# Two layers of cross-attention with experts: the softmax computed on keys-by-queries scores, built batch by batch

## Chip, cores and metric

One core of one Trainium2 chip runs the whole program in one launch. The metric is the device time of one execution in microseconds (us).

## The reference, cut to what matters

Two layers run one after the other on `x` (16 batches of 128 tokens, width 256). Each layer is a cross-attention with a residual, then a mixture of experts with a residual. The change touches only the attention:

```python
# per layer: h = layernorm(x)
# q = h @ Wq.T + bq ; k, v = ctx @ Wk.T + bk, ctx @ Wv.T + bv   16 heads of 16; layer 0 turns q and k by rope
# s = q @ k.T / 4                      per batch and head: 128 queries x 128 keys
# layer 1: s = where(mask == 0, -big, s)   over keys
# x = x + softmax(s) @ v @ Wo.T + bo
```

Results have to hold fp32 accuracy, which is why products are made of a high and a low part of each operand.

## The kernel before, in words

**Staging.** A layer's attention works in four blocks of four batches (`N` = 512 tokens). Groups are numbered i = 0 to 15 in a block: group i is four heads (two per half `u`) of batch i // 4. Engines are programmed by hand, each with its own order, and meet by semaphores; `attend(n, build)` exists once for each engine (TensorE L1386, ScalarE L647, VectorE L1056, GpSimd `outputs` L445).

**Path of one group.** `scores` (L1328) multiplies queries by keys, K = 32 rows at a time, in fp32, into banks 0 to 3; two heads of a 32-row stripe are told apart by `k_half`, which holds the keys twice, each time with the other head's rows at zero. In layer 1 a product with `mask_b` adds the mask (L1352). `shifted` (L1027, VectorE) takes the maximum over keys, negated, and for even groups also adds it to the scores (L1037). `exps` (L627, ScalarE) takes the exponential: in one instruction for even groups, and in four with the maximum as bias for odd ones (L636). `turned` (L1358) transposes the four 128x128 blocks on TensorE (L1364). ScalarE copies them to a high half in fp16 (L654), VectorE makes the low half (L1063), and `weighed` (L1368) multiplies both by the values, which are split in three bf16 parts and carry a column of ones (`VW` = 50 columns a head), into banks 6 and 7. ScalarE copies the sums out (L644), VectorE takes the reciprocal of the denominator (L1043), GpSimd adds the three parts and divides (L453 to L458).

**Blocks.** The last four groups of a block also build the next block's keys and queries (`unit`, L1301), GpSimd does the last step of rope (L443), and after them come the values (L1317). In layer 0 every key or query unit needs two products, one with the weights and one with the weights of the partner column. At a block's end all its outputs are transposed (L1406), split (L668, L1076), multiplied by Wo and added to `xres` (L1086). `attend` is a hardware loop on ScalarE, VectorE and GpSimd.

Of the kernel before, what the change touches and what calls it, by code (L numbers as in the profile page):

```python
# [18 lines left out]
VW = 50  # L19
RING, RINGT = 6, 3  # L20
# [15 lines left out]
def program(nc, x, ctxT, maskrow, tab_in, ident_in, aw, ab, arow, rw, rrow, fw, sort_in, empty_in, sorted_x, summed, out):  # L36
# [7 lines left out]
    with ctx:  # L44
# [20 lines left out]
        first_row = sb(ctx, "first_row", [P, P], BF16)  # L65
        mask_b = sb(ctx, "mask_b", [P, B * S], BF16)
        half_col = sb(ctx, "half_col", [P, 2], F32)
# [24 lines left out]
        aw_hi = sb(at, "aw_hi", [P, 6, KT, D], F32R)  # L92
        aw_lo = sb(at, "aw_lo", [P, 6, KT, D], F32R)
        rope_b = sb(at, "rope_b", [P, 2, N], F32)
        qk = sb(at, "qk", [P, 2, N], F32)
        k_half = sb(at, "k_half", [P, KT, 2, N], F32)
        q_full = sb(at, "q_full", [P, KT, N], F32)
        gap = sb(at, "gap", [P, 7 * 1024], F32)
        v32 = sb(at, "v32", [P, 2, 2, D], F32)
        v_parts = sb(at, "v_parts", [P, BLK, HEADS, VW], BF16)  # L100
        gap2 = sb(at, "gap2", [P, 2 * 1024], F32)
        probT_hi = sb(at, "probT_hi", [P, RINGT, N], F16)
        probT_lo = sb(at, "probT_lo", [P, RINGT, N], F16)
        nmax = sb(at, "nmax", [P, 2, HEADS], F32)
        rden = sb(at, "rden", [P, 2, HEADS // 2], F32)
        o_raw = sb(at, "o_raw", [P, 2, HEADS // 2, VW], F32)
        o_sb = sb(at, "o_sb", [P, BLK, HEADS, HD], F32)
        oT_hi = sb(at, "oT_hi", [P, KT, N], F32R)
        oT_lo = sb(at, "oT_lo", [P, KT, N], F32R)
        st = ExitStack()  # L110
        prob = sb(st, "prob", [P, RING, N], F32)
        st.close()

# [50 lines left out]
        s_half = sem("s_half")  # L164
# [4 lines left out]
        s_rope = sem("s_rope")  # L169
        s_wsplit = [sem(f"s_route_split{l}") for l in range(2)]  # L170

        def stage_sems(names, l):
# [5 lines left out]
                          "proj", "qk", "kfirst", "ksecond", "vps", "v32", "vhi", "vones", "vres", "vmid", "vlo",  # L178
                          "score", "max", "sub", "exp", "pT", "phi", "plo", "pv", "ocopy", "oadd", "rden", "olast",
                          "o", "oT", "ohi", "olo", "wo", "xadd", "xbo"], l)  # L180
# [16 lines left out]
        NW = [6, 4]  # L197
        JT = [2, 1]


        V_W, O_W = [4, 2], [5, 3]
        W_ORDER = [[2, 3, 0, 1, 4, 5], [1, 2, 0, 3]]
        KV_WEIGHTS = 2
        UNIT_W = [[(2, 3), (2, 3), (0, 1), (0, 1)], [(1,), (1,), (0,), (0,)]]
        GROUPS = BLK * NG
# [10 lines left out]
        def four_by_two(c):  # L216
            return (o_raw[:, c % 2].rearrange("p (u m) w -> p u m w", u=2),
                    o_sb[:, c // 2].rearrange("p (u c m) d -> p c u m d", u=2, c=2)[:, c % 2])
# [5 lines left out]
        def _(sp):  # L224
# [6 lines left out]
            sp.dma_start(aw_raw[:, 0, :], aw[0][:, W_ORDER[0][0], :]).then_inc(AT[0]["aw_in0"], 16)  # L231
            sp.dma_start(aw_raw[:, 1, :], aw[0][:, W_ORDER[0][1], :]).then_inc(AT[0]["aw_in1"], 16)
# [15 lines left out]
            for l in range(2):  # L248
# [6 lines left out]
                for i, w in enumerate(W_ORDER[l]):  # L255
# [4 lines left out]
                    sp.dma_start(aw_raw[:, i % 2, :], aw[l][:, w, :]).then_inc(a[f"aw_in{i % 2}"], 16)  # L260
# [22 lines left out]
                sp.wait_ge(a["xadd"], 2 * NBLK)  # L283
# [36 lines left out]
        def _(pool):  # L320
# [91 lines left out]
            for r in range(NG):  # L412
                nc.gpsimd.memset(first_row[32 * r:32 * r + 1, :], 1.0).then_inc(s_set, 1)
# [7 lines left out]
            for l in range(2):  # L421
# [23 lines left out]
                def outputs(n, build):  # L445

                    for c in range(2 * BLK - 1):
                        if build and l == 0:
                            for i in {4: (0,), 5: (1, 2), 6: (3,)}.get(c, ()):
                                rotate(n + 1, i)  # L450
# [1137 lines left out]
```

## Time and profile before

| | us |
|---|---|
| median of 3 runs | 1118.29 (1117.19 to 1121.87) |
| the profiled execution | 1119.13 |
| its span, first to last instruction | 1117.3 |
| first scores to last residual, layer 0 | 49.1 to 233.5 |
| first scores to last residual, layer 1 | 600.6 to 772.1 |
| TensorE matmul busy, of the span | 952.8 (85%) |
| VectorE, ScalarE, GpSimd busy | 776.6, 581.0, 436.6 |
| mean granted TensorE clock | 0.940 of 2.4 GHz |

Busy shares are means over stages with different limits. TensorE's matmuls overlap in the records (each lasts until its result is written), so the time from one start to the next tells more than the mean of one. Some matmul records can be missing. A fp32 matmul that isn't a transpose stands as two instructions in the trace: the four products of a `scores` call are eight records.

### The profile page before, as it was taken

How to read it: one execution, taken by the hardware profiler on the slowest of the kernel's cores; microseconds unless marked ns; L12 is line 12 of the kernel's file. 1: busy time of each engine (PE TensorE's matmuls, PEld its weight loads, DVE VectorE, ACT ScalarE, POOL GpSimd, SP SyncE). 2: the span in 40 equal slices, each digit the busy share in tenths (PEclk: the TensorE clock that was granted, in tenths of full speed). 3: DMA queues.
4: the chain of work that ended last, by engine and by line, in shares of the span. 5: the costliest groups of instructions: out<-in, count | busy, mean ns of one | idle time of the engine just before them, and what ended most of it. 6: DMA issues, size and time to landing. Idle time of an engine off the chain costs nothing.

```text
span 1117.3 us, 20415 instructions
## 1 busy us (share of the span) xinstructions
PE 952.8 (85%) x6981; PEld 825.7 (74%) x6981; DVE 776.6 (70%) x1538; ACT 581.0 (52%) x1112; POOL 436.6 (39%) x479
## 2 busy tenths in 40 slices
PE   2798878748987999999837888885989999999995
PEld 2577667536877999999825767665678888888885
DVE  5688787866664777777655687795686666667665
ACT  5375675745234667667546877874622232322221
POOL 1465556240663666666415444334012212212210
PEclk9989999859998999999956899996899999999999
DMA  3300750010325888888540000001000001000002
GB/s 129 110 21 1 189 144 1 1 61 1 128 82 193 237 231 233 227 221 233 119 134 1 20 20 1 1 2 43 15 15 29 28 14 28 17 26 28 14 0 76
DMA packets 44281, 85.81 MB, mean 77 GB/s; under 512 B 4161, under 2 KB 31041, under 8 KB 44097
## 3 DMA queue, kind: packets, MB, share of 16 engines
q0 software_dynamic: 14784, 46.44, 15.1%
q1 hardware_dynamic: 29440, 38.61, 11.9%
q8 instruction: 37, 0.61, 0.2%
q14 instruction: 20, 0.16, 0.0%
HBM read 64.25 MB, written 20.79 MB: 76 GB/s over the span
## 4 chain that ended last, share of the span: by engine, by line
PE 48%; DVE 20%; ACT 11%; issue 9%; DMA 7%; POOL 4%; DVEq 0%; ACTq 0%; POOLq 0%
PE bank L1179 31%; PE bank L1215 8%; DMA w_raw<-in_fw,w_idx 4%; DVE nmax L1034 3%; PE bank L1274 3%; DVE probT_lo L1063 2%; PE bank L1364 2%; DVE prob L1037 2%; POOL sorted_x L375 2%; ACT xn L512 2%; DMA summed<-y_sb,tile_to 2%; ACT probT_hi L654 1%; ACT o_raw L644 1%; PE bank L1343 1%; ACT w_hi L533 1%
## 5 line engine op out<-in xcount | busy, mean ns | idle before, releaser
L1179 PE MATMUL bank<-xT_hi,w_hi 128*128 128x512 f32 x352 | 139.9, 398 | 2.2 <-DVE hid L964 2.2
L581 ACT ACTIVATE act_sb<-bank 128x512 f32<-128x512 f32 x88 | 52.6, 598 | 167.8 <-PE bank L1179 167.7
L1179 PE MATMUL bank<-xT_lo,w_hi 128*128 128x512 f32 x352 | 139.3, 396 | 0.0
L1179 PE MATMUL bank<-xT_hi,w_lo 128*128 128x512 f32 x352 | 139.1, 395 | 0.0
L964 DVE TENSOR_TENSOR hid<-bank,act_sb 128x512 f32<-128x512 f32 x88 | 60.8, 691 | 107.3 <-ACT act_sb L581 107.1
L332 POOL TENSOR_TENSOR w_hi<-w_raw,zero_col 128x768 fp32r<-128x768 f32 (+1 forms) x20 | 31.9, 1595 | 262.9 <-PE bank L1215 236.8
L951 DVE SCALAR_TENSOR_TENSOR xres<-bank,gate,xres 128x256 f32<-128x256 f32 x320 | 132.6, 476 | 0.8 <-PE bank L1215 0.8
L1364 PE MATMUL bank<-ident,prob 128*128 128x128 f32 x512 | 86.2, 298 | 31.9 <-DVE probT_lo L1063 26.0
L1063 DVE TENSOR_TENSOR probT_lo<-bank,probT_hi 128x512 f16<-128x512 f32 x128 | 88.0, 687 | 32.4 <-ACT probT_hi L654 31.8
L1179 PE MATMUL bank<-xsT_hi,w_hi 128*128 128x256 f32 x368 | 106.5, 289 | 2.3 <-DVE xsT_lo L918 1.5
L1215 PE MATMUL bank<-w_hi,hid_hi 128*128 128x256 f32 x352 | 99.5, 283 | 6.2 <-DVE hid_lo L972 6.2
L1179 PE MATMUL bank<-xsT_hi,w_lo 128*128 128x256 f32 x368 | 103.4, 281 | 0.0
L586 ACT ACTIVATE hid_hi<-hid 128x512 fp32r<-128x512 f32 x88 | 55.7, 633 | 91.7 <-PE bank L1215 53.7
L1179 PE MATMUL bank<-xsT_lo,w_hi 128*128 128x256 f32 x368 | 103.3, 281 | 0.0
L1364 PEld LDWEIGHTS bank<-ident,prob 128*128 128x128 f32 x512 | 60.7, 150 | 56.5 <-issue 29.6
L1215 PE MATMUL bank<-w_hi,hid_lo 128*128 128x256 f32 x352 | 99.6, 283 | 0.0
L1215 PE MATMUL bank<-w_lo,hid_hi 128*128 128x256 f32 x352 | 99.3, 282 | 0.0
L394 POOL DMA_INDIRECT summed<-y_sb,tile_to x46 | 84.7, 1842 | 21.1 <-DMA summed<-y_sb,tile_to 10.9
L1034 DVE TENSOR_REDUCE nmax<-bank 128x4 f32<-128x512 f32 x128 | 85.7, 675 | 8.4 <-PE bank L1352 6.0
L654 ACT ACTIVATE probT_hi<-bank 128x512 f16<-128x512 f32 x128 | 77.3, 604 | 19.5 <-PE bank L1364 19.2
L359 POOL DMA_INDIRECT w_raw<-in_fw,w_idx x46 | 49.8, 1083 | 94.8 <-ACT y_sb L550 35.2
L533 ACT ACTIVATE w_hi<-w_raw 128x1536 fp32r<-128x1536 f32 x46 | 68.2, 1484 | 33.4 <-DMA w_raw<-in_fw,w_idx 33.3
(199 smaller groups left out, 2763.5 us busy)
## 6 DMA issues: line engine op xcount, KB each, us to landing
w_raw<-in_fw SPq DMA_DIRECT2D x18, 384.0 KB, 3.0
sorted_x<-empty_row SPq DMA_DIRECT2D x2, 2967.0 KB, 21.4
xs<-sorted_x SPq DMA_DIRECT2D x23, 258.0 KB, 3.4
ctx_raw<-in_ctxT SPq DMA_DIRECT2D x8, 512.0 KB, 5.2
aw_raw<-in_aw SPq DMA_DIRECT2D x10, 256.0 KB, 3.8
summed<-empty_row SPq DMA_DIRECT2D x1, 2304.0 KB, 29.6
xres<-in_x SPq DMA_DIRECT2D x4, 512.0 KB, 5.7
xn_all<-summed SPq DMA_DIRECT2D x4, 512.0 KB, 5.9
```

The source lines that it names most:

```text
L394: nc.gpsimd.indirect_dma_start(out=summed, out_offset=bass.IndirectOffsetOnAxis(ap=tile_to[:, j, c:c + 1], axis=0), in_=y_sb[:, j % 2, c, ...
L533: nc.scalar.activation(w_hi4[s][:], w_raw4[s], ACT.Copy).then_inc(TS["w_hi"], 1)
L581: nc.scalar.activation(act_sb[:, (ls * J + j) % 2, :], bank[2 * ((ls * J + j) % 2) + 1][:], ACT.Silu).then_inc(f["act"], 1)
L586: nc.scalar.activation(hid_hi[:, ls % 2, j, :], hid[:, (ls * J + j) % 2, :], ACT.Copy).then_inc(f["hhi"], 1)
L654: nc.scalar.activation(probT_hi[:, i % RINGT, :], bank[4 + i % 2][:], ACT.Copy).then_inc(a["phi"], 1)
L951: nc.vector.scalar_tensor_tensor(out=rows, in0=bank[4 + 2 * (ls % 2) + sub // 2][:, D * (sub % 2):D * (sub % 2 + 1)], scalar=gate[:, ds(it ...
L964: nc.vector.tensor_tensor(hid[:, r, :], bank[2 * r][:], act_sb[:, r, :], ALU.mult).then_inc(f["hid"], 1)
L1034: nc.vector.tensor_reduce(mx, grp, AX.X, ALU.max, negate=True).then_inc(a["max"], 1)
L1063: nc.vector.tensor_tensor(probT_lo[:, i % RINGT, :], bank[4 + i % 2][:], probT_hi[:, i % RINGT, :], ALU.subtract).then_inc(a["plo"], 1)
L1179: last = nc.tensor.matmul(dst, lh, rh, start=(i == 0), stop=(i == len(pairs) - 1))
L1215: last = nc.tensor.matmul(dst, h, w, start=(i == 0), stop=(i == len(pairs) - 1))
L1364: last = nc.tensor.transpose(bank[4 + i % 2][:, S * h:S * (h + 1)], prob[:, i % RING, S * h:S * (h + 1)], ident[:])
```

## The change

The softmax's second half no longer transposes probabilities. Scores are computed twice: queries by keys only for the maximum, and keys by queries, onto which TensorE itself adds the negated maximum before the exponential. The probabilities come out already turned, and the values are the stationary operand, 32 columns a head in fp32. Work goes by batch (16 steps and two to drain), unrolled on every engine; keys, queries and values of a later block are built two items a step. In layer 0 the partner product is gone: VectorE exchanges neighbouring rows instead.

```diff
+        def build_at(b):
+            early = {0: (1, K0, K1), 1: (1, Q0, Q1), 2: (1, V0, V1)}
+            if b in early:
+                return early[b]
+            n, s = divmod(b, BLK)
+            if s == 3 and n + 2 < NBLK:
+                return n + 2, K0, V0
+            if s == 0 and n + 1 < NBLK:
+                return n + 1, K1, V1
+            if s == 1 and n + 1 < NBLK:
+                return n + 1, Q0, Q1
+            return None
...
 # SP: one more load
+                sp.dma_start(mask_col[:], maskrow.rearrange("o (b t) -> (o t) b", t=S),
+                             allow_slow_non_contiguous=True).then_inc(s_in, 16)
...
 # GpSimd: outputs, value_parts gone; clears v_full (8 x 16 x 32 a partition) and low_col in each layer
+                nc.gpsimd.memset(v_full[:], 0.0).then_inc(a["vset"], 1)
+                nc.gpsimd.memset(v_full[:, :, :, :, HD], 1.0).then_inc(a["vset"], 1)
...
 # ScalarE
+                def attend():
+                    context_high(1)
+                    low_copy(0)
+                    for b in range(B + 2):
+                        if b < B:
+                            exponential(b, 0)
+                            exponential(b, 1)
+                        if 1 <= b <= B:
+                            output_copy(b - 1)
+                        if b < B:
+                            exponential(b, 2)
+                            exponential(b, 3)
+                        if b >= 2:
+                            output_high(b - 2)
+                        made, before = build_at(b), build_at(b - 1) if b else None
+                        for item in before[1:] if before and l == 0 else ():
+                            if item not in (V0, V1):
+                                unit_out(before[0], item)
+                        for item in made[1:] if made and l == 1 else ():
+                            if item not in (V0, V1):
+                                unit_out(made[0], item)
+                        if b in (2, 5):
+                            context_high(2 + b // 4)
+                        if b + 1 < B:
+                            low_copy(b + 1)
...
 # VectorE
+                    dve.wait_ge(a["rope"], 3 * u + 2)
+                    nc.vector.stream_shuffle(rope_b[:, r], rope_b[:, r], PAIR).then_inc(a["rope"], 1)
...
+                def attend():
+                    lowest(0)
+                    for b in range(B + 2):
+                        if b + 1 < B:
+                            lowest(b + 1)
+                        if b >= 2:
+                            output_low(b - 2)
+                        made = build_at(b)
+                        if made:
+                            made_item(made[0], made[1])
+                        if 1 <= b <= B:
+                            output(b - 1)
+                        if b >= 2:
+                            residual(b - 2)
+                        if made:
+                            made_item(made[0], made[2])
...
 # TensorE, scores(b): queries by keys, then the mask in layer 1
+                    if b >= 1:
+                        pe.wait_ge(a["lowcopy"], b)
+                    if b >= 3:
+                        pe.wait_ge(a["o"], b - 2)
...
+                    for u in range(KT):
+                        for h in range(2):
+                            for r in range(NG):
+                                rows = slice(32 * r, 32 * r + 32)
+                                at_col = 256 * u + S * h
+                                last = nc.tensor.matmul(bank[r][:, at_col:at_col + S], q_half[rows, n % 2, u, h, cols],
+                                                        k_full[rows, n % 2, u, cols], start=(u == 0 and h == 0),
...
 # scores_turned(b): waits for all exponentials of b-1 and for VectorE's reads of banks 4 and 5
+                    if b >= 1:
+                        pe.wait_ge(a["exp"], NG * b)
...
+                            nc.tensor.matmul(bank[4 + r][:, 256 * u:256 * u + 256], k_full[rows, n % 2, u, cols],
+                                             q_half[rows, n % 2, u, :, cols], start=(u == 0), stop=False)
+                    pe.wait_ge(a["lowcopy"], b + 1)
...
+                            last = nc.tensor.matmul(bank[4 + r][:, S * h:S * (h + 1)], pick[rows, h, :],
+                                                    low_row[rows, b % 2, :], start=False, stop=(h == GRP - 1))
...
 # weighed(b)
+                    for pair in range(2):
+                        for u in range(KT):
+                            for q in range(4):
+                                r, j = 2 * pair + q // 2, q % 2
+                                last = nc.tensor.matmul(bank[0][32 * q:32 * q + VW, S * (2 * u + pair):S * (2 * u + pair + 1)],
+                                                        v_full[:, n % 2, c, 8 * u + 2 * r + j, :],
+                                                        prob[:, b % 2, r, S * (2 * u + j):S * (2 * u + j + 1)],
+                                                        start=True, stop=True)
...
+                def attend():
+                    scores(0)
+                    lows_turned(0)
+                    for b in range(B + 2):
+                        made = build_at(b)
+                        if b + 1 < B:
+                            scores(b + 1)
+                        if b < B:
+                            scores_turned(b)
+                        if 1 <= b <= B:
+                            weighed(b - 1)
+                        if b >= 2:
+                            output_turned(b - 2)
+                        if made:
+                            pe.wait_ge(a["exp"], NG * b + 1)
+                            make_item(made[0], made[1])
+                        if 1 <= b <= B:
+                            turned_back(b - 1)
+                        if b >= 2:
+                            projected(b - 2)
+                        if made:
+                            pe.wait_ge(a["exp"], NG * b + 2)
+                            make_item(made[0], made[2])
+                        if b + 1 < B:
+                            lows_turned(b + 1)
```

What the new names stand for. `lowest` (VectorE): four maximum reductions of a bank of 512 columns. `lows_turned`: one transpose of the maxima; `low_copy` (ScalarE): a copy of 128 columns. `exponential` (ScalarE): one bank of 512 columns, with a bias column. `output_copy` (ScalarE): bank 0, 512 columns. `turned_back`: four transposes. `output` (VectorE): a reciprocal of 16 columns and a product of 256. `output_turned`: two transposes; `output_high` (ScalarE), `output_low` (VectorE): 256 columns; `projected`: six products of 256 columns; `residual` (VectorE): 256 columns. A key or query unit is six products of 512 columns on TensorE; in layer 0 VectorE follows with two operations of 512 columns and the shuffle, GpSimd subtracts, and for queries ScalarE writes two copies of 512 columns (`unit_out`); in layer 1 ScalarE writes a key unit with one and Q1 with two, VectorE Q0 with two. A value item is twelve products of 256 columns and two additions of 256 on VectorE.

## Rows read from the trace of the kernel before

**Rows 1.** The page: busy time by engine, and the chain's shares by engine
```profile
PE 952.8 (85%) x6981; PEld 825.7 (74%) x6981; DVE 776.6 (70%) x1538; ACT 581.0 (52%) x1112; POOL 436.6 (39%) x479
PE 48%; DVE 20%; ACT 11%; issue 9%; DMA 7%; POOL 4%; DVEq 0%; ACTq 0%; POOLq 0%
```
**Rows 2.** The chain in order of time: start, us, what; first piece of blocks
```profile
122.88 2.81 PE bank L1179 x12
168.88 2.81 PE bank L1179 x12
...
632.89 1.66 PE bank L1179 x6
641.02 2.97 PE bank L1179 x24
...
674.01 1.66 PE bank L1179 x6
```
**Rows 3.** Windows: stretch, length, busy us and instructions by engine, PEclk, DMA
```profile
138.50:184.50 46.00, 38.41 (x361) 31.77 (x362) 37.75 (x69) 29.67 (x71) 22.80 (x32) 1.00 0.37 92
184.50:218.00 33.50, 25.87 (x280) 21.38 (x280) 28.62 (x53) 24.46 (x63) 14.59 (x23) 1.00 0.00 1
218.00:231.50 13.50, 8.71 (x67) 7.83 (x65) 5.53 (x13) 5.76 (x10) 3.70 (x9) 0.50 0.01 1
...
602.00:620.00 18.00, 15.21 (x100) 11.01 (x98) 12.90 (x20) 12.18 (x30) 16.18 (x11) 0.54 0.00 0
...
674.00:715.20 41.20, 34.95 (x369) 28.71 (x369) 32.10 (x59) 32.12 (x76) 17.83 (x29) 1.00 0.01 1
```
**Rows 4.** Groups by line and form, VectorE: busy us, mean ns, idle before
```profile
L1063 DVE TENSOR_TENSOR probT_lo<-bank,probT_hi 128x512 f16<-128x512 f32 x128 | 88.0, 687 | 32.4 <-ACT probT_hi L654 31.8
L1034 DVE TENSOR_REDUCE nmax<-bank 128x4 f32<-128x512 f32 x128 | 85.7, 675 | 8.4 <-PE bank L1352 6.0 <-PE bank L1343 2.4
...
L1005 DVE SCALAR_TENSOR_TENSOR qk<-bank,bias_col,rope_tab 128x512 f32<-128x512 f32 x16 | 12.0, 749 | 6.0 <-PE bank L1179 5.8
L1043 DVE RECIPROCAL rden<-o_raw 128x8 f32<-128x8 f32 x64 | 11.9, 193 | 8.4 <-ACT o_raw L644 8.4
...
L799 DVE TENSOR_TENSOR rt<-bank,logit 128x256 f32<-128x256 f32 x1 | 0.4, 425 | 0.2 <-ACT logit L701 0.2
```
**Rows 5.** The same view, ScalarE
```profile
L654 ACT ACTIVATE probT_hi<-bank 128x512 f16<-128x512 f32 x128 | 77.3, 604 | 19.5 <-PE bank L1364 19.2
...
L601 ACT ACTIVATE ctx_hi<-ctx_raw 128x1024 fp32r<-128x1024 f32 x8 | 8.5, 1067 | 0.0
...
L610 ACT ACTIVATE q_full<-bank,bias_col 128x512 f32<-128x512 f32 x8 | 5.5, 684 | 3.1 <-PE bank L1179 3.1
...
L701 ACT ACTIVATE logit<-bank 128x256 f32<-128x256 f32 x1 | 0.4, 385 | 0.5 <-PE bank L1467 0.5
```
**Rows 6.** Timeline: start, us, engine, line, operation, count, idle before
```profile
66.19 1.13 PE L1343 MATMUL bank<-k_half,q_full 32*128 32x256 f32 x8
67.26 0.66 PE L1364 MATMUL bank<-ident,prob 128*128 128x128 f32 x4
...
142.90 1.16 PE L1343 MATMUL bank<-k_half,q_full 32*128 32x256 f32 x16
...
147.05 1.14 ACT L636 ACTIVATE prob<-bank,nmax 128x128 f32<-128x128 f32 x4
...
149.40 1.09 PE L1364 MATMUL bank<-ident,prob 128*128 128x128 f32 x8
```
**Rows 7.** Timeline at the first scores and first work after, both layers
```profile
49.10 1.16 PE L1343 MATMUL bank<-k_half,q_full 32*128 32x256 f32 x16 [0.87 <-DVE v L1023]
...
233.53 1.39 DVE L745 BATCH_NORM_STATS2 stats<-xres 128x6 f32<-128x256 f32 x4
...
600.59 0.70 PE L1343 MATMUL bank<-k_half,q_full 32*128 32x256 f32 x4 [0.88 <-DVE v L1023]
...
772.07 1.39 DVE L745 BATCH_NORM_STATS2 stats<-xres 128x6 f32<-128x256 f32 x4
```

More of the change, by code:

```diff
@@ L18 @@
 NG = HEADS // GRP
-VW = 50
-RING, RINGT = 6, 3
+VW = 32
 E0, E1 = 8, 16
@@ L163, in program @@
         s_first = sem("s_first")
-        s_half = sem("s_half")
         s_x = [sem(f"s_x{n}") for n in range(NBLK)]
@@ L475, in _ @@
-                outputs(NBLK - 1, False)
-                pool.wait_ge(a["xadd"], 2 * NBLK)
+                context_low(a, 1)
+                for b in range(B):
+                    made = build_at(b)
+                    for item in made[1:] if made and l == 0 else ():
+                        if item not in (V0, V1):
+                            rotate(made[0], item)
+                    if b in (2, 5):
+                        context_low(a, 2 + b // 4)
+                pool.wait_ge(a["xadd"], B)
@@ new lines, in values @@
+                def values(m, item):
+                    h = (V0, V1).index(item)
+                    if m == 0:
+                        dve.wait_ge(a["vset"], 2)
+                    dve.wait_ge(a["vps"], 2 * m + h + 1)
+                    src = bank[unit_bank(l, m, item)]
+                    for c in range(2):
+                        nc.vector.tensor_tensor(v_full[:, m % 2, 2 * h + c, :, 0:HD],
+                                                src[:, D * c:D * (c + 1)].rearrange("p (h d) -> p h d", h=HEADS),
+                                                bv_row[l][:].rearrange("p (h d) -> p h d", h=HEADS),
+                                                ALU.add).then_inc(a["v"], 1)
@@ L1101, in _ @@
-                    values(0)
+                    for item in (K0, K1):
+                        unit_build(0, item)
+                    weights_low(range(2, NW))
+                    for item in (Q0, Q1):
+                        unit_build(0, item)
+                    for item in (V0, V1):
+                        values(0, item)
                     first_constants()
@@ new lines, in values @@
+                def values(m, item):
+                    pe.wait_ge(a["ctx_lo"], m + 1)
+                    h = (V0, V1).index(item)
+                    for c in range(2):
+                        rows = slice(P * (2 * h + c), P * (2 * h + c + 1))
+                        last = products(bank[unit_bank(l, m, item)][:, D * c:D * (c + 1)],
+                                        (lambda k: ctx_hi[:, k, rows], lambda k: ctx_lo[:, k, rows]),
+                                        (lambda k: aw_hi[:, V_W, k, :], lambda k: aw_lo[:, V_W, k, :]))
+                    last.then_inc(a["vps"], 1)
```

687 lines of the change are left out of this document (299 added, 388 removed).

## The prediction

> **What bounds the kernel now.** I read the page first: TensorE is busy 85% of the span but holds only 48% of the chain, VectorE 20%, ScalarE 11%, and "issue" 9% [rows 1]. So outside the experts no engine is the bound alone. The chain in order of time then gives the period of the part that changes: the same piece returns at 122.88 and 168.88, so a layer-0 block of four batches takes 46.0 us (11.5 a batch), and at 632.89 and 674.01 in layer 1, 41.1 us (10.3 a batch) [rows 2]. The windows show what fills it: in 46.0 us VectorE is busy 37.75, TensorE 38.41 (its records overlap), ScalarE 29.67 [rows 3]. The groups name VectorE's part: 128 low halves of 0.69 and 128 maxima of 0.675 us, idle mostly for ScalarE's copy [rows 4]. A group travels ScalarE, TensorE, ScalarE, VectorE, TensorE. The change removes that trip for the probabilities, so I ask which loop replaces it.
>
> **Prices.** Four transposes take 0.66 and eight 1.09 us, so 0.11 for each further fp32 instruction of 128 columns. Sixteen score instructions of 256 columns on four 32-row stripes take 1.16 us where eight on two stripes take 1.13 (1.07 to the next start): stripes run side by side, 0.22 per instruction within one [rows 6]. Split products cost 2.81/12 = 0.23 us at 512 columns and 2.97/24 = 0.124 at 256 [rows 2]. VectorE: 0.64 for each maximum in a row, 0.42 for 256 columns, 0.75 for a rope operation, 0.2 for a reciprocal [rows 4]. ScalarE: 0.60 to 0.68 for 512 columns from PSUM, 0.385 for 256 [rows 5]; four in a row take 1.14 where one would be 0.375, so starts come some 0.09 closer than durations [rows 6]. I give 0.2 to 0.25 from a last matmul's start to its reader, 0.05 between other engines.
>
> **One step without building**, times from the start of scores(b+1):
> - scores: 32 instructions of 128 columns, eight a stripe, the columns of the sixteen-instruction call: 1.0.
> - scores_turned(b): 16 of 256 columns, four a stripe, 0.87, and 32 of 128, eight a stripe, 0.88: ends 2.75.
> - ScalarE: two exponentials, output_copy, two exponentials, output_high: 1.2 + 0.5 + 1.2 + 0.45 from 3.0 to 6.4.
> - VectorE: output_low 0.45, to 6.9; then output(b-1), 0.65, which scores(b+2) also wait for, at 7.55.
> - TensorE: projected, six of 256 columns, 0.75, to 7.65; lows_turned, 0.35 to its reader; ScalarE's low_copy 0.3. Next start: 8.3.
>
> Hidden: the four maxima (2.6, from 1.2 to 3.8), the products with the values, the transposes back (copy at 4.7, TensorE otherwise idle until 6.9), the residual. By engine time alone a step would be about 5.2 us of TensorE and 4.2 of VectorE: this step is a chain of three engines, not a full engine. ScalarE's order makes it so: low_copy stands behind output_high, TensorE's lows_turned behind projected.
>
> **The products with the values.** No row shows 32-column products in different column groups. If the four groups run side by side, as the stripes do, 8 x 0.11 = 0.9 us; one after another, 32 x 0.11 = 3.5. I take 0.9, since the row stripes [rows 6] are the nearest case. Output_copy has 0.3 us of room; past that each microsecond is a microsecond of step.
>
> The Trainium skill speaks on both sides here. "TensorE: Matmul & The Clock Gate", Part 3, gives 2.38 times for three column tiles, by which the products would take some 1.1 us and stay hidden; the same part says that weight loads overlap running matmuls only when the row group differs, which in column groups it doesn't, by which they would go one after another. No run here shows either yet.
>
> **Building steps** (nine of sixteen). Layer 0, two key or query units: VectorE does the first one's two rope operations and shuffle (2.2) before output(b-1): next start 9.8, +1.5; the second one's rope operations end at 11.7, and scores_turned wait for them 0.9 longer: +2.4. Key with value: +1.8. After a query step ScalarE's four copies (2.9) delay low_copy: +1.4; in step 2 they and a 1.07 us ctx_hi [rows 5], +2.4. The shuffle has no row: 0.5 (half a rope operation and a start) to 0.75, I take 0.7, as nearest to a two-operand pass. Steps 0 and 1 lack the drain work, so I add nothing. Sum: 4 x 1.8 + 3 x 2.4 + 2 x 1.4, 17 us. Layer 1: ScalarE has key units, TensorE's 1.4 us item lies between projected and lows_turned: +1.4 for key with value (four), +2.8 for the two query steps, 2.1 for step 2, 1 for steps 0 and 1: 14 us; the mask adds 0.25 to each step's scores (four side by side, one pass of 512 columns).
>
> **The sum.** Layer 0: start 4.5 (scores 1.0, maxima 2.6, turn and copy 0.7), fifteen steps 124.5, building 17, the last step with the drain 12.8 (7.2 to projected, then 5.6 in line: products, copy, transposes, division, split, Wo, residual): 159. TensorE stands at 1.2 GHz near starts and ends, as in 602 to 620 (0.54) and 218 to 231.5 (0.50) [rows 3]; some 3.7 us of a step are TensorE's on the path and double there, for about ten and a few us: +6, so 165. Before it is 233.5 - 49.1 = 184.4 [rows 7]: -19.4. Layer 1: 4.7 + 15 x 8.55 + 14 + 12.8 + 6 = 166, before 171.5 [rows 7]: -5.5. In front of layer 0, 24 products of 512 columns go, 24 x 0.23 = 5.6 [rows 2]: -5.6. In front of layer 1 the values move ahead of the layernorm, 24 x 0.124 = 3.0 saved, about 1.5 given back since VectorE must add them first: -1.5. Total -32. Clearing v_full on GpSimd is paid at nothing: in layer 0 it lies under the first layernorm; in layer 1 only if it takes over 5 us would VectorE's values wait, at most some 3 us. The mask_col load, 2048 pieces of 4 bytes on SP's queue ahead of the other constants: nothing; it is wanted only after VectorE's units; at worst 10 us once. Fewer GpSimd passes: nothing, its bound was elsewhere.
>
> Profiled execution 1119.13 - 32 = 1087.1; it stands 0.84 above the median of 1118.29. I predict 1087. Below half a per cent (5.6 us) a measurement of this kernel can't tell a change from none.
>
> **Rivals.**
> 1. *Column groups one after another.* weighed ends 2.6 us later, output_copy waits for it, the last two exponentials, output_high, output_low, projected and the next scores follow: 3.0 + 1.2 to 6.4 instead of 4.2 for the copy's start, +2.15 a step in 32 steps, +69: 1156, slower by 3%. It decides from about 2.2 us for weighed: 0.9 + 0.3 of room + 32/32. For it: no row shows column groups. Against it: the stripes' row. The second rule of the skill above is this rival.
> 2. *TensorE falls to 1.2 GHz in the steps without building.* Seven steps and the drain of each layer lose 3.7 us each, 7 x 2 x 3.7 = 52: 1139, slower by 2%. For it: from 218 the granted clock was 0.50 while TensorE worked on transposes and short products, and in my step only 52% is other matmuls, with a hole from 3.7 to 6.9 us. Against it: from 184.5 to 218, with score products only 1.1 us at a time, it held 1.00 nearly throughout [rows 3]. [...]
> 3. *The chain is shorter or the builds cheaper.* If ScalarE's and TensorE's starts come closer than I allow, 0.5 us a step: 1070.
> 4. *It all nets out.* A microsecond of unlisted restarts and waits a step, 32 us: 1119. Against it: the gaps are already in the prices from starts.
>
> **How the numbers follow.** Forecast 0.60, its own range 1068 to 1107 (0.6 us a step either way, shuffle and exponential bounds in it); rival 1 0.13; rival 2 0.11; rival 3 0.10; rival 4 0.06. From 1064 to 1142 lie the forecast, rivals 3 (most), 4 and 2: about 0.82. Faster: 0.60 + 0.10 and a part of rivals 2 and 4 that falls short, 0.73; same 0.06; slower 0.21.
>
> **What the profile after would show.** Right: steps of about 8.3 us (8.6 in layer 1) from batch 10 on, four maxima under the turned scores, and scores waiting for ScalarE's low_copy; weighed of 16 products within 1.1 us; VectorE's shuffle before each slow start in layer 0's first ten steps; granted clock 1.00 in most of both stages. Wrong: start-to-start of 0.11 between all 32 instructions of weighed, ScalarE's output_copy waiting for them (rival 1); a granted clock of 0.50 in the last third of each stage (rival 2); a step below 7.5 would say that the chain through low_copy isn't the path, one above 9.5 that I missed a wait.

## The result and the profile after

Measured on the chip of the first comparison, the changed kernel takes 1108.74 us (1101.79 to 1111.49, 4 executions) against 1120.08 for the kernel before on the same chip: ratio 0.9893, 95% interval 0.9853 to 0.9933. Run again later, unaltered, beside another set of runs of before, it takes 1102.31 (1098.76 to 1109.16), ratio 0.9855 (0.9795 to 0.9915). It is faster by 1.1 to 1.5%, 11 to 18 us by the medians, where 32 were forecast; the forecast time of 1087 lies below every execution of it. Ratios leave out executions in the slower of the chip's two states; in all that follows that is one, of e10_zero_now.

The first lines of the page of the changed kernel answer to [rows 1]: busy time by engine, then the chain's shares.

```profile
PE 934.6 (84%) x8517; PEld 817.2 (74%) x8517; DVE 672.6 (61%) x1398; ACT 471.9 (43%) x790; POOL 321.8 (29%) x262
...
PE 60%; ACT 16%; DVE 12%; issue 5%; POOL 4%; DMA 3%; DVEq 0%; POOLq 0%; ACTq 0%
```

VectorE lost 104 us of work, ScalarE 109 and GpSimd 115, and the span fell by 8 and 18: none of the three was the bound by itself. The chain moved to TensorE, from 48% to 60%. Where the span changed, between the marks of [rows 7] (first scores, first layernorm statistics after the attention), in us:

| stage | before | forecast | after | difference | after, second trace |
|---|---|---|---|---|---|
| start to first scores | 49.1 | -5.6 | 44.6 | -4.5 | -5.0 |
| layer 0 attention | 184.4 | -19.4 | 174.9 | -9.5 | -15.2 |
| between the attentions | 367.1 | -1.5 | 372.8 | +5.7 | +5.1 |
| layer 1 attention | 171.5 | -5.5 | 173.2 | +1.7 | -1.1 |
| rest | 345.2 | 0 | 344.1 | -1.1 | -1.4 |
| sum | 1117.3 | -32.0 | 1109.6 | -7.7 | -17.7 |

So three lines failed, both attentions and the stage between. The windows over the two attentions, changed kernel, with the columns of [rows 3] (length, busy us of TensorE's matmuls, its weight loads, VectorE, ScalarE and GpSimd, then the granted clock, DMA share and GB/s):

```profile
44.55:219.50 174.95, 136.90 (x2144) 115.06 (x2144) 90.33 (x189) 68.21 (x129) 31.78 (x21) 0.90 0.24 58
592.30:765.50 173.20, 139.07 (x2208) 117.05 (x2208) 71.34 (x146) 68.08 (x129) 7.04 (x3) 0.90 0.03 8
```

The forecast wanted a granted clock of 1.00 in most of both. It is 0.90, and the windows of single steps say where it goes. These are batches 13 to 15 of layer 0, none of which builds anything:

```profile
173.10:183.90 10.80, 7.31 (x134) 5.85 (x132) 5.09 (x12) 4.46 (x11) 0.00 (x0) 1.00 0.01 2
183.90:187.30 3.40, 3.19 (x48) 2.97 (x52) 1.29 (x3) 0.16 (x1) 0.00 (x0) 0.50 0.02 5
187.30:194.10 6.80, 4.69 (x93) 3.65 (x89) 2.89 (x7) 3.46 (x7) 0.00 (x0) 1.00 0.00 0
194.10:197.50 3.40, 3.40 (x56) 3.18 (x52) 1.83 (x4) 0.00 (x0) 0.00 (x0) 0.50 0.02 5
197.50:204.40 6.90, 4.60 (x89) 3.60 (x85) 2.09 (x6) 3.46 (x7) 0.00 (x0) 0.99 0.00 0
204.40:207.80 3.40, 3.40 (x60) 3.11 (x56) 0.00 (x0) 0.67 (x2) 0.00 (x0) 0.50 0.02 5
```

Once a step the clock falls to 1.2 GHz and comes back, just where `scores` and `scores_turned` run (in the last window, after the last scores, `scores_turned` and `weighed`), which are all TensorE and all on the path. From the scores of batch 12 on every step of both layers has such a fall, but for the one shown next; between the start and there the clock is 1.00 but for two falls a layer. Before each fall lies a stretch in which TensorE waits for ScalarE and VectorE. The chain in order of time shows one step that escaped, from 175.95 to 184.11, and the start of the step after it, which didn't. In the changed kernel L1345 is `scores`, L1370 and L1376 are `scores_turned`, L632 `exponential`, L637 `output_copy`, L641 `output_high`, L1064 `output_low`, L1177 all split products (here `projected`), L1393 `lows_turned` and L628 `low_copy`:

```profile
175.95 1.17 PE bank L1345 x32
177.13 0.86 PE bank L1370 x16
177.99 0.94 PE bank L1376 x32
178.93 0.03 issue
178.95 1.27 ACT prob L632 x2
180.22 0.49 ACT o_turned L637
180.71 1.16 ACT prob L632 x2
181.86 0.28 ACT oT_hi L641
...
182.17 0.43 DVE oT_lo L1064
182.60 0.04 issue
182.65 0.99 PE bank L1177 x6
183.63 0.12 PE bank L1393
183.76 0.02 issue
183.78 0.29 ACT low_row L628
184.07 0.04 issue
184.11 2.07 PE bank L1345 x29
```

The first is the forecast's chain link by link, 8.16 us where it said 8.3, with VectorE's `output` off the path. In the second the scores take 2.07 us instead of 1.17, and the whole step 9.68.

### The profile page after: what moved, and what is told of

The parts are those of the page before. It is cut to its first block, busy times and chain, and to the rows that moved or that the text cites. A ratio compares the mean times of both kernels' runs of the same rounds, so it can differ in the third digit from the quotient of the medians.

```text
span 1109.6 us, 21972 instructions
## 1 busy us (share of the span) xinstructions
PE 934.6 (84%) x8517; PEld 817.2 (74%) x8517; DVE 672.6 (61%) x1398; ACT 471.9 (43%) x790; POOL 321.8 (29%) x262
## 3 DMA queue, kind: packets, MB, share of 16 engines
q0 software_dynamic: 14784, 46.44, 15.6%
## 4 chain that ended last, share of the span: by engine, by line
PE 60%; ACT 16%; DVE 12%; issue 5%; POOL 4%; DMA 3%; DVEq 0%; POOLq 0%; ACTq 0%
PE bank L1177 33%; PE bank L1213 8%; ACT prob L632 6%; PE bank L1272 5%; PE bank L1345 4%; PE bank L1370 3%; PE bank L1376 3%; POOL sorted_x L399 2%; ACT xn L512 2%; DMA w_raw<-in_fw,w_idx 2%; ACT o_turned L637 1%; DVE oT_lo L1064 1%; DVE shift L752 1%; PE bank L1409 1%; DVE hid_lo L963 1%
## 5 line engine op out<-in xcount | busy, mean ns | idle before, releaser
L1177 PE MATMUL bank<-xT_hi,w_hi 128*128 128x512 f32 x352 | 139.7, 397 | 2.2 <-DVE hid L955 2.2
L1177 PE MATMUL bank<-xT_lo,w_hi 128*128 128x512 f32 x352 | 139.7, 397 | 0.0
L1177 PE MATMUL bank<-xT_hi,w_lo 128*128 128x512 f32 x352 | 139.4, 396 | 0.0
L1049 DVE TENSOR_REDUCE low_col<-bank 128x4 f32<-128x512 f32 x128 | 79.4, 683 | 64.8 <-PE bank L1351 44.3
L1177 PE MATMUL bank<-xsT_hi,w_hi 128*128 128x256 f32 x368 | 106.8, 290 | 2.3 <-DVE xsT_lo L909 1.5
L1177 PE MATMUL bank<-xsT_hi,w_lo 128*128 128x256 f32 x368 | 103.6, 282 | 0.0
L1177 PE MATMUL bank<-xsT_lo,w_hi 128*128 128x256 f32 x368 | 103.6, 281 | 0.0
L904 DVE TENSOR_TENSOR w_lo<-w_raw,w_hi 128x1536 fp32r<-128x1536 f32 x46 | 80.6, 1752 | 2.1 <-ACT w_hi L533 2.1
L1177 PEld LDWEIGHTS bank<-xT_lo,w_hi 128*128 128x128 f32 x352 | 66.3, 188 | 16.0
L1177 PEld LDWEIGHTS bank<-xT_hi,w_hi 128*128 128x128 f32 x352 | 66.4, 189 | 14.7 <-issue 2.3
L1213 PEld LDWEIGHTS bank<-w_hi,hid_hi 128*128 128x128 f32 x352 | 66.6, 189 | 12.7 <-DVE hid_lo L963 9.1
```

The costliest lines, as they stand in the source:

```text
L904: nc.vector.tensor_tensor(w_lo4[s][:], w_raw4[s], w_hi4[s][:].bitcast(F32), ALU.subtract).then_inc(TS["w_lo"], 1)
L1049: nc.vector.tensor_reduce(low_col[:, b % 2, 32 * r:32 * r + GRP], bank[r][:].rearrange("p (h t) -> p h t", h=GRP), AX.X, ALU.max, negate=T ...
L1177: last = nc.tensor.matmul(dst, lh, rh, start=(i == 0), stop=(i == len(pairs) - 1))
L1213: last = nc.tensor.matmul(dst, h, w, start=(i == 0), stop=(i == len(pairs) - 1))
```

## The experiments

Four questions: does the clock account for the loss (theory 1) or a wait that the forecast missed (theory 2); what is a stall of 4 us in batch 4 (theory 3, the read of instructions behind the zero writes); what does GpSimd's queue cost (theory 4). Ratios are to the kernel before on the same chip. In each chip's set of runs before stood at another median (1118.5, 1126.6 and 1119.9 us), so ratios compare better than times.

| run | us, median | ratio to before (95%) | layer 0 | layer 1 | step without building |
|---|---|---|---|---|---|
| changed | 1108.7 | 0.9893 (0.9853 to 0.9933) | 174.9 | 173.2 | 8.2 to 10.0 |
| e1_warm | 1092.9 | 0.9777 (0.9725 to 0.9828) | 162.4 | 164.0 | 8.13, 8.36 |
| e2_lows_early | 1092.3 | 0.9762 (0.9713 to 0.9811) | 169.0 | 162.4 | 7.8 to 9.5 |
| e3_chain_short | 1051.7 | 0.9401 (0.9345 to 0.9457) | 151.1 | 136.0 | 6.59, 6.80 |
| e4_zero_later | 1104.2 | 0.9854 (0.9802 to 0.9906) | 170.6 | 173.6 | 8.2 to 10.5 |
| e5_serial | 1143.8 | 1.0154 (1.0099 to 1.0209) | 193.8 | 189.2 | 9.9 to 11.5 |
| e6_ctx_first | 1103.4 | 0.9797 (0.9738 to 0.9855) | 168.7 | 171.6 | 8.1 to 10.4 |
| e7_short_ctx | 1049.2 | 0.9342 (0.9284 to 0.9400) | 148.0 | 137.5 | 6.59, 6.80 |
| e8_high_only | 1066.9 | 0.9485 (0.9426 to 0.9545) | 152.6 | 149.2 | 7.13, 7.34 |
| e9_values_after | 1107.6, one run | | 175.0 | 170.4 | 8.2 to 10.4 |
| e10_zero_now | 1104.4 | 0.9823 (0.9749 to 0.9898) | 180.2 | 171.6 | 8.1 to 10.4 |
| e11_as_changed | 1102.3 | 0.9855 (0.9795 to 0.9915) | 169.2 | 170.4 | 8.1 to 10.4 |

Layers and steps are from each run's one trace, from the start of one batch's scores to the next; steps right behind a query build are left out. Two steps with a comma are those of layer 0 and layer 1. In layer 0 of e3, e7 and e8 one such step, from 154.7, 151.7 and 154.7 us on, still holds a fall of the clock and takes 8.07, 8.14 and 8.76. The time of e10_zero_now is the median of all four executions, its ratio that of three.

### Filler in TensorE's holes (e1_warm)

```diff
+                def warm(b, count):
+                    if b + 1 < B:
+                        pe.wait_ge(a["max"], NG * (b + 2))
+                    for i in range(count):
+                        nc.tensor.matmul(bank[3][:], aw_hi[:, O_W, i % 2, 0:P], xT_hi[:, i % 2, 0:N], start=True, stop=True)
...
                             output_turned(b - 2)
+                            if not made and b + 1 < B:
+                                warm(b, 2)
...
                             turned_back(b - 1)
+                        if b >= 2 and not made and b + 1 < B:
+                            warm(b, 4)
```

> The changed kernel with filler products in its steps without building: two of 512 columns on TensorE after output_turned and four after turned_back, into bank 3, which nobody reads then; results unchanged. Theory 1 (the lower granted clock in steps without building is what lengthened them from about 8.4 to 9.8-10.0 us): the dips to 0.50 between batches 10 and 15 go, those steps take 8.3 to 8.8 us in both layers, the kernel is 8 to 15 us faster than the changed kernel (about 1094 to 1100). Theory 2 (the steps are long by a wait that the forecast missed, and the clock only follows idle time): the granted clock rises or not, the steps stay at 9.5 us or more, and the kernel is unchanged or up to 5 us slower.

The filler is useless work, six products of 512 columns in each step that builds nothing. The window over three such steps, whose columns are as above:

```profile
159.70:184.10 24.40, 22.31 (x393) 17.74 (x393) 11.69 (x24) 10.37 (x21) 0.00 (x0) 1.00 0.01 3
```

24.40 us are three steps of 8.13 at a granted clock of 1.00. Time at 1.2 GHz fell from 33.5 to 13.7 us in layer 0 and from 34.1 to 13.7 in layer 1; 10.2 us of what is left lie at the start and the end of each layer, where the forecast had put its 6 us, and 3.4 in one step in the middle, from 120.0 and from 645.6 us on. Layer 1 gained 9.2 us. Layer 0 gained 12.5, of which 3.7 are not the clock: this trace has no stall in step 5 (9.58 instead of 14.67) but a longer step 1 (11.35 instead of 9.94). So the clock cost 8.8 and 9.2 us against this trace. Against the second trace of the changed kernel it is 7.6 (169.2 to 162.4, with step 1 0.8 longer) and 6.4. Theory 1 holds: 14 to 18 us. What in a step lets the clock fall isn't separated by this run, since the filler both shortens TensorE's longest pause and gives it more to do. More work on an engine made the kernel 0.8 to 1.2% faster.

### One order on ScalarE (e8_high_only)

```diff
+                        if b >= 2:
+                            output_high(b - 2)
                         if b < B:
                             exponential(b, 2)
                             exponential(b, 3)
-                        if b >= 2:
-                            output_high(b - 2)
```

> Only ScalarE's output_high moves ahead of the last two exponentials of a step, TensorE's order stays. By the forecast's chain (scores, turned scores, exponentials, output_high, output_low, projected, lows_turned, low_copy) it takes output_low and projected off the path: the step without building is scores 1.0, turned 1.75, exponentials and copies 3.4, low_copy 0.3, or 6.8 instead of 8.2, if the chain is what bounds it; the gain is 1.3 us a step in 30 steps, and the half clock goes where TensorE's hole of 1.2 us goes: 1050 to 1070. Rival (the clock alone was the cost, the two orders only matter together): 1095 to 1109.

The chain of one step, in the same columns:

```profile
172.60 0.94 PE bank L1376 x32
173.54 0.02 issue
173.56 1.26 ACT prob L632 x2
174.83 0.49 ACT o_turned L637
175.32 0.28 ACT oT_hi L641
175.60 0.02 issue
175.62 0.43 DVE oT_lo L1064
176.06 0.21 issue
176.27 0.96 PE bank L1177 x6
```

The 1.16 us of the second pair of exponentials left the chain: step 7.13 instead of 8.16. That is 1.0 us. The expectation of 6.8 had taken `output_low` and `projected` off the path; the chain above still goes through both, so that part of it failed. The clock came with it: TensorE's hole shrank, and the time at 1.2 GHz fell to 17.1 and 10.2 us without a filler. Together that is 42 us by the medians of two chips, 3.7 to 4.1% by the ratios. The rival (the clock alone) is out, since e1, with the clock, kept 8.13.

### The other order, and both (e2_lows_early, e3_chain_short)

```diff
 # e2: TensorE
                             turned_back(b - 1)
+                        if b + 1 < B:
+                            lows_turned(b + 1)
                         if b >= 2:
                             projected(b - 2)
 # e2: ScalarE (and the old places of both removed)
                             exponential(b, 2)
                             exponential(b, 3)
+                        if b + 1 < B:
+                            low_copy(b + 1)
                         if b >= 2:
                             output_high(b - 2)
 # e3: the same on TensorE; on ScalarE
+                        if b >= 2:
+                            output_high(b - 2)
+                        if b < B:
+                            exponential(b, 2)
+                        if b + 1 < B:
+                            low_copy(b + 1)
+                        if b < B:
+                            exponential(b, 3)
```

> Order alone: lows_turned goes ahead of projected on TensorE, low_copy ahead of output_high on ScalarE. If the path of a step runs through output_high, output_low, projected, lows_turned, low_copy to the next scores (the forecast's chain), a step without building loses 0.65 us (turn and copy) and the steps after a query build in layer 0 lose up to 1.4 more, -15 to -22 us over both layers: about 1088 to 1095. If the path doesn't run there but through a full engine or the clock, under 5 us.

> As e2_lows_early, and output_high goes ahead of the third exponential, low_copy between the third and fourth. By the forecast's chain a step without building is then scores_turned 1.75, exponentials with copies 3.7, scores 1.0: about 6.5 to 7 us, building steps 8.5 to 9.5, and TensorE's share of such a step rises from 0.6 to 0.8, so theory 1 adds that its clock stays at 1.00: about 1050 to 1070 in all. If theory 2 holds (another wait is the path), no faster than e2_lows_early.

By itself the earlier turn of the maxima gives 0.4 us a step at full clock (7.77, where 0.65 was expected) and leaves the falls of the clock (9.4 beside 7.8). It is worth 0.9 to 1.3% by the ratios, most of it in layer 1, where the turn now comes ahead of the unit that TensorE builds (query steps 9.9 instead of 11.0 to 11.9); in layer 0 most steps that build grew, from 9.6 to 10.2. Both together give steps of 6.59 and 6.80, one fall of the clock left in the steps without building, and 6% over before.

### Column groups one after another (e5_serial)

```diff
-                    for pair in range(2):
-                        for u in range(KT):
-                            for q in range(4):
+                    for q in range(4):
+                        for pair in range(2):
+                            for u in range(KT):
```

> Weighed issues the same 16 products (32 records) with the column group outermost, so that neighbours in time share a column group; nothing else changes. Rival 1 of the prediction, made true on purpose. If it is the order over the four column groups that lets the products run side by side, weighed goes from 1.08 us to about 32 x 0.11 = 3.5 us, ScalarE's output copy waits for it, and a step grows by about 2.15 us, 32 steps: near 1175 us, less some 15 if the busier TensorE keeps its clock: 1160. If the products run side by side in any order, or are cheap for another reason, nothing changes: 1109.

Two lines of TensorE's timeline of this run: the products that add the maximum, and `weighed` (start, us, count):

```profile
84.52 1.10 PE L1376 MATMUL bank<-low_row,pick 32*128 32x128 f32 x32
85.55 2.46 PE L1409 MATMUL bank<-prob,v_full 128*32 128x128 f32 x32
```

Only the order differs, and at full clock `weighed` takes 2.46 us in this view; in the changed kernel it takes 1.08. So interleaving the four column groups is what makes it cheap, which is what rival 1 turned on. Its price was high: 2.46 us for 32, not 3.5. The run is slower than before by 1.5%, and than the changed kernel by 2.6 to 3.0% (from the ratios), 29 to 33 us, where rival 1 said 69. It takes 1143.8 us and not the 1160 to 1175 expected.

### GpSimd's queue (e6_ctx_first, e7_short_ctx)

```diff
-                add_bias(2 * l, bo_row[l], a)
                 context_low(a, 1)
+                add_bias(2 * l, bo_row[l], a)
```

> GpSimd makes the low half of the second context block before it adds the output bias to the residual, in both layers. Theory 4 (the forecast's 'steps 0 and 1 add nothing' missed GpSimd's queue): in the changed kernel the first built unit waits for GpSimd until 56.6 us, 4.62 of bias and 2.31 of low half after the first scores; the low half first takes TensorE's wait of 1.6 us at 56.6 away and VectorE's of 3.5, so layer 0's steps 0 and 1 shrink by 2 to 4 us together: 1105 to 1107. Rival: the wait moves to the residual of batch 0 or to the key weights, nothing is won: 1109.

> The shortened chain (lows_turned ahead of projected, output_high ahead of the third exponential, low_copy ahead of the fourth) with the context's low half ahead of the bias on GpSimd. In the shortened-chain run the first built unit waited for GpSimd for 2.9 us of TensorE and step 1 took 13.0. Theory 4: step 1 falls to about 10, 1051.7 becomes 1048 to 1049. Rival: the step is bound by VectorE's rope pass whatever comes first: 1051.5.

e7 has the order of e3 and this edit. First the chain of the changed kernel at its first built unit, which shows the wait:

```profile
49.56 4.62 POOL xres L350 x2
54.18 2.31 POOL ctx_lo L364
56.50 0.14 issue
56.63 1.64 PE bank L1177 x6
58.27 0.03 issue
58.30 0.75 DVE qk L1017
```

The step of batch 0 builds the next block's keys, and those wait for GpSimd, which first adds its bias blocks. From the scores of batch 1 to those of batch 2, which wait for that step's end, it was 9.5 to 13.0 us in the ten traces with that order. It is 9.50 and 8.18 in the two without it. In the shortened chain that is 13.01 to 8.18, while the step before it is 0.9 longer. In the unshortened one the first two steps together take 15.1 instead of 15.6 us, where 2 to 4 us less were expected: the unit starts only 0.5 us earlier behind the scores, since it then waits for the first exponential, and VectorE's rope passes follow on the path in either case. Second, and unforeseen, the stretch in front of layer 1's scores, from the load of the summed rows on, fell to 34.6 and 34.1 us, where the ten other traces of changed kernels have 37.2 to 38.5. The chain of the changed kernel shows the place; the rows are one instruction of VectorE, 4 elements wide, in four blocks of the layernorm:

```profile
563.70 0.16 DVE shift L752
567.30 1.23 DVE shift L752
572.02 1.05 DVE shift L752
577.70 0.17 DVE shift L752
```

and GpSimd's timeline at that time:

```profile
566.15 2.35 POOL L350 TENSOR_TENSOR xres<-xres,bo_row 128x1024 f32<-128x1024 f32 x1 [9.88 <-ACT xn L512]
570.70 2.36 POOL L350 TENSOR_TENSOR xres<-xres,bo_row 128x1024 f32<-128x1024 f32 x1 [2.20 <-ACT xn L512]
```

Each long `shift` starts inside a bias pass and ends with it (566.15 + 2.35 = 568.50; 567.30 + 1.23 = 568.53). In e6, where GpSimd does no bias pass there, all four take 0.16 or 0.17. The Trainium skill ("SBUF — State Buffer", "Who interferes with whom") says that a VectorE instruction with two SBUF inputs contends with a GpSimd instruction that reads SBUF; the trace agrees. This is 1.95 of the 3.3 us; the rest is not itemised. The same happens in front of layer 0's experts, and already in the kernel before, whose rows follow: there the instruction takes 2.36 and 2.72 us (2.63 and 2.71 in the changed kernel) under GpSimd's passes of 2.75 us over the expert weights.

```profile
238.49 2.36 DVE L761 SCALAR_TENSOR_TENSOR shift<-meanvar,rstd 128x4 f32<-128x4 f32 x1
244.35 2.72 DVE L761 SCALAR_TENSOR_TENSOR shift<-meanvar,rstd 128x4 f32<-128x4 f32 x1
```

```profile
238.08 2.75 POOL L332 TENSOR_TENSOR w_hi<-w_raw,zero_col 128x1536 fp32r<-128x1536 f32 x1 [13.58 <-DMA w_raw<-in_fw]
```

The times agree in sign: 0.9797 against 0.9893 and 0.9855, and 0.9342 against 0.9401 for the shortened chain; the intervals overlap, so the gain is read from the traces and the times don't show it.

### Values back behind the layernorm (e9_values_after)

```diff
 # VectorE, layer 1 (TensorE likewise)
-                    for item in (V0, V1):
-                        values(0, item)
                     ln_dve(2, tiles_back)
...
                     for item in (Q0, Q1):
                         unit_build(0, item)
+                    for item in (V0, V1):
+                        values(0, item)
```

> Layer 1's first values go back behind the layernorm and the first queries, on TensorE and on VectorE; all else as changed. It tests the forecast's term 'front of layer 1 -1.5'. The forecast: from the load of the summed rows to the first scores the stage grows from 37.9 by 1.5 us or more (24 products of 256 columns return to the path, 3 to 5.5 us at the clock of that stretch, and VectorE's two value passes ahead of the layernorm, 1.5, go): 39.4 to 41.5. Rival (the stage is set by VectorE under GpSimd's bias passes, TensorE has room): 36.4 to 37.9.

The stretch is 38.2 us, 0.3 above the changed kernel's and inside the spread of the other traces. By the expectation it is neither case cleanly: the 1.5 or more of the forecast's term isn't there, and the upper end of the rival's is passed by 0.3. With the bias passes where they are, the place of the first values is worth nothing that this one trace shows.

### The stall in batch 4 (e4_zero_later, e10_zero_now, e11_as_changed)

TensorE's weight loads in the changed kernel, ten of the 32 of `weighed`, then a pause that no semaphore explains:

```profile
93.15 0.36 PEld L1409 LDWEIGHTS bank<-prob,v_full 128*32 128x32 f32 x10
97.71 0.59 PEld L1409 LDWEIGHTS bank<-prob,v_full 128*32 128x32 f32 x22 [4.20 <-issue]
```

The edits: e4 lets SP issue the three writes of zeros after the tenth residual, e10 loads their source row before the context loop, so that they start 3.6 us earlier; e11 is the changed kernel.

```diff
 # e4
+                    sp.wait_ge(a["xadd"], 10)
                     sp.dma_start(empty_row[:], empty_in).then_inc(TS["const_in"], 16)
 # e10: that load moved ahead of
                 for n in range(NBLK - 1):
                     sp.wait_ge(a["ctx_lo"], n + 1)
```

> The three large writes of zeros to memory (8.2 MB) wait until batch 9 of layer 0 has its residual. Theory 3 (the 4.2 us gap at 93.5 us, in which TensorE stood still in the middle of weighed with every input ready, is a fetch of instructions behind these writes): no such gap at batch 3 and 4, perhaps one of 2 to 5 us after batch 10, where the writes now are; the total 0 to 5 us less. Rival: the gap stays at batch 3 to 4 (it has nothing to do with the writes), total unchanged.

> SP loads the row for the zero writes before it waits for the third context block, so the 5.3 MB of zero writes are issued at about 83.3 us instead of 87.7; nothing else moves. In the traces so far the packet of instructions that was read at 85 to 88 us in seven runs was missing there in the two whose TensorE stood still for 4 us in batch 4's products with the values (the changed kernel and the run with the column group outermost); there it came at 95 and 98, with the writes in flight. Theory 3 (the read of instructions falls behind the writes): now the writes are always in flight at 85 to 88, the read is late and TensorE stands still for about 4 us around 90 to 97 in this trace: 1109 or a few us above, against 1105 without the stall. Rival (the stall has another cause): none appears in this trace, and 1105.

> The changed kernel once more, unaltered, on the chip of these runs, with its own trace. Theory 1 (the clock): again one piece of about 3.4 us at 0.50 of the clock in nearly every step without building, at other places than in the first trace, steps of 8.2 and of 9.6 to 10.2 and nothing between. Theory 3: the 4 us stall of TensorE near 94 us is there or not, with the late packet of instructions or without it. Time 1100 to 1112.

In e10 the same ten weight loads come, and the pause is longer:

```profile
94.01 0.36 PEld L1410 LDWEIGHTS bank<-prob,v_full 128*32 128x32 f32 x10
99.91 1.05 PEld L1410 LDWEIGHTS bank<-prob,v_full 128*32 128x32 f32 x22 [5.54 <-issue]
```

The view of the DMA queues from 84 to 94 us tells the two kinds apart. In the changed kernel (first below) it lists one queue's packets; in the same program's second trace a packet of 16 KB of instructions too, and there TensorE doesn't pause:

```profile
q1 hardware_dynamic: 1962, 2.38, 82.9%
```

```profile
q1 hardware_dynamic: 2058, 2.45, 80.7%
q8 instruction: 1, 0.02, 0.6%
```

Four traces have the pause (changed, e5, e9, e10); in three the packet is missing in that stretch and comes at 95 to 97 us, while the three writes of zeros (8.2 MB by their sizes on the page; the 5.3 in e10's expectation leaves one out) are in flight, and in e5, whose steps are longer, the gap is between the packets at 84.1 and 98.3. The eight without a pause have a packet at 85 to 88. The two traces of one program, e11 and the first, show that it is chance whether the packet gets in before the writes. e10, with the writes started earlier on purpose, has the pause, as theory 3 said; e4, with the writes moved away, has none, neither there nor behind the moved writes. Between the traces the step that holds the pause takes 14.67 and 14.64 us (changed, e9) where e11 has 9.57, and the attention of layer 0 takes 175 us where e4, e6 and e11 have 168.7 to 170.6. The times of whole runs don't resolve it: the executions of e10 (1091.5 to 1115.4) enclose those of e11. e10's profiled execution, 1115.35, is 1% above its own median, so I read the pause from it and no time. That the late read is what stops TensorE fits twelve traces, but it stays an inference: no row names it as releaser.

## Why the prediction was wrong

The sign and the chain were right; the size was not, by a factor of two to three. Its own range of 1068 to 1107 misses the first measurement by 2 us and holds the second, 1102.3. By its steps:

- **The step without building: right.** 8.16 and 8.13 us measured at full clock, 8.3 forecast; in layer 1 8.36, forecast 8.55. Scores, turned scores, exponentials and copies are within 0.2 of their terms.
- **The products with the values: right.** 1.08 us for 32 records (0.81 from the first start to the last), 0.9 forecast. The second rule cited of the Trainium skill ("TensorE: Matmul & The Clock Gate", Part 3), that weight loads overlap only when the row group differs, would have made them serial; here they share one row group and run side by side as long as neighbours in time differ in column group. Rival 1 is out, and e5 shows it would have been real: 2.46 us, slower than before.
- **The clock: the step that failed.** The forecast wrote "TensorE stands at 1.2 GHz near starts and ends" and gave 6 us a layer; that part was near (with the filler 10.2 us at 1.2 GHz at start and end of a layer). It took 1.00 for everything between, since the score stage before had held it [rows 3]. But TensorE's rows of before from 138.5 to 184.5 show only two pauses over 1 us (1.09 and 1.42), and the new step has one of 1.24 us every 8, ahead of the projection, with two of 0.4 to 0.5 beside it. In e1 the long one is 0.31, in e8 0.24 and in e3 gone, and so are nearly all falls; in e2 it stays (1.29), and the falls with it. That points at the pause; but TensorE's share of a step rose in the same runs, so which of the two counts isn't shown. The price is 14 to 18 us, more than the 17 or 9 by which the two traces' attentions missed, because the rest, stall aside, came out 2.6 and 2.0 us below the forecast (162.4 and 164.0 for 165 and 166). Rival 2 named this mechanism and priced it at 3.7 us a step; it is 1.5 to 1.7 in this trace and up to 2.4 in the other unshortened ones (10.54 in e4), as the clock is low for about a third of a step and not all of it. So the truth lay between forecast and rival, and each took it as all or nothing.
- **Building: the sum was near, the parts weren't.** e1's layer 0, with one fall left (1.7 us), gives 21.2 us over fourteen steps of 8.13, where 17 were forecast. The start's terms add up to 4.3 and not to the 4.5 written; it took 4.7 to 5.6 in layer 0. "Steps 0 and 1 lack the drain work, so I add nothing" failed: step 1 waits for GpSimd's bias passes, 11.35 us in e1. Query units cost 1.4 instead of 2.4, keys with values 1.4 instead of 1.8 (9.53 and 9.56 against 8.13); after a query step it is +1.7 for the forecast's 1.4. The shuffle was priced 0.7 and takes 0.73.
- **Front of layer 0: nearly right.** -4.5 and -5.0 for -5.6.
- **Front of layer 1: wrong sign.** -1.5 forecast, +1.8 measured (36.0 to 37.9). "Fewer GpSimd passes: nothing, its bound was elsewhere" is the sentence that failed. Without its value work GpSimd reaches the bias passes while VectorE is in the layernorm; before, it did nothing in that stretch but wait. With those passes moved the stretch is 34.6, 1.4 below before. That it meets the forecast's -1.5 is no proof of its reason: putting the values back cost only 0.3 (e9).
- **Not foreseen, and partly open.** The stall, 4.2 us in one trace and none in the next. And 4 us between the attentions that no run explains (2.8 in the second trace): from the first statistics to the first expert product 26.2 instead of 24.8, then 81.4 instead of 79.7, 227.4 instead of 226.5. The second of these moved between 80.3 and 88.4 from trace to trace with no edit in it, so part of it may not be the kernel's.

The wide range of 1064 to 1142 held the result with rivals 2 and 4 in it; 1108.7 lies between the forecast and rival 4 (1119), but rival 4's reason, an unlisted microsecond in every step, is not what the traces show.

## What to carry to other kernels

When a change empties several engines and leaves TensorE in a chain with waits, price the clock by the step: look for the hole in the new order and ask whether the work behind it is on the path. Then shorten the hole, not the engines: one copy placed ahead of two exponentials was worth more than twice the whole change (3.7 to 4.1% beside 1.1 to 1.5%). And follow an engine that is relieved to what it starts earlier; its next pass may land on somebody's critical instruction.

## What was not expected of the hardware

- The granted clock fell and rose again within one step of 8 to 10 us, step after step, and useless products on TensorE (six of 512 columns a step) removed it: 0.8 to 1.2% faster with more work.
- Products of 32 columns in four column groups run side by side when issued in turn, 1.08 us for 32 records, and in 2.46 us when one group is issued after another.
- A 4-element VectorE instruction of 0.16 us took 1.05 and 1.23 us under a GpSimd pass of 2.36 us, and 2.36 and 2.72 under passes of 2.75.
- TensorE stood for 4 to 5.5 us in the middle of a row of products in four of twelve traces, those in which a packet of instructions came late, three of them with 8.2 MB of zeros being written at that time.
